# A macaron layer on one core: when PE ranks the tokens of batch 2, and whether VectorE adds the mix before or after its side piece

## The reference

```python
def attn(x):
    Q, K, V = (jnp.einsum('bne,hde->hbnd', x, W) for W in (Wq, Wk, Wv))
    scores = jnp.einsum('hbnd,hbmd->hbnm', Q, K) * scale
    w = jax.nn.softmax(scores, axis=2)
    mean = jnp.mean(jnp.einsum('hbnm,hbmd->hbnd', w, V), axis=0)
    return mean @ fc_w.T + fc_b
def ffn(x):
    scores = sigmoid(x @ gate_w)
    _, selected = top_k(scores + expert_bias, 2)   # weights: scores of the two, normalised
    shared = silu(x @ shared_gate_w) * (x @ shared_up_w) @ shared_down_w
    for e in range(16):
        routed = routed + comb[:, e:e+1] * (silu(g_e(x)) * u_e(x) @ experts_down[e])
    return shared + routed
x = x + 0.5 * ffn(layernorm(x))
x = x + attn(layernorm(x))
x = x + 0.5 * ffn(layernorm(x))
```

## Time and profile before

| | |
|---|---|
| median of 3 runs | 512.28 us (509.96, 512.28, 513.18) |
| the profiled execution | 512.53 us, of which its span is 511.3 us |
| PE busy in the span | 442.7 us, 87% |
| granted TensorE clock, mean | 0.956 of full speed |
| attention stage | about 165 to 396 us of the span |

### The profile page before, as it was taken

One profiled execution on the slowest core, in us unless ns is written; L12 is line 12 of the kernel. 1 busy time (PEld: TensorE's weight loads), 2 busy tenths in 40 slices (PEclk: granted clock), 3 DMA queues, 4 the chain that ended last, 5 costly groups with the idle time before them and its releaser, 6 DMA issues. The chain is left out here.

```text
span 511.3 us, 10128 instructions
## 1 busy us (share of the span) xinstructions
PE 442.7 (87%) x2951; PEld 394.0 (77%) x2951; DVE 342.4 (67%) x1053; ACT 265.7 (52%) x708; POOL 278.3 (54%) x322
## 2 busy tenths in 40 slices
PE   1676799999787899999999999989979888999982
PEld 1345699899666789988889888979868677899972
DVE  6589575565448575458646875675685786777778
ACT  4855376676523455543544454435434663577750
POOL 5267875565064643386344746738657167266660
PEclk9977699999989999999999999999998988999995
DMA  8672375576632100011000111104001466366968
GB/s 295 242 226 92 114 210 160 189 207 130 160 94 63 53 21 1 1 52 35 28 12 22 53 31 50 57 3 141 31 33 62 153 222 213 102 189 188 303 227 254
DMA packets 44468, 60.33 MB, mean 118 GB/s; under 512 B 6080, under 2 KB 36800, under 8 KB 44416
## 3 DMA queue, kind: packets, MB, share of 16 engines
q1 hardware_dynamic: 34688, 37.11, 23.2%
q0 software_dynamic: 7584, 20.98, 13.7%
q10 hardware_dynamic: 2144, 1.60, 1.0%
HBM read 34.75 MB, written 24.91 MB: 117 GB/s over the span
## 5 line engine op out<-in xcount | busy, mean ns | idle before, releaser
L2099 POOL TENSOR_TENSOR e_sp<-raw,e_sp 128x512 fp32r<-128x512 f32 x48 | 62.2, 1296 | 69.5 <-ACT e_sp L1163 69.0
L400 PE MATMUL bank<-v_sp,e_sp 128*128 128x256 f32 x576 | 78.1, 286 | 2.4 <-DVE x_sb L1703 2.0
L400 PEld LDWEIGHTS bank<-v_sp,e_sp 128*128 128x128 f32 x576 | 75.4, 193 | 6.2 <-issue 2.8
L400 PE MATMUL bank<-g_sp,xT 128*128 128x512 f32 x288 | 75.5, 398 | 0.1
L2063 POOL DMA_INDIRECT raw<-xn_dram,gather_at x47 | 45.6, 971 | 30.9 <-PE bank L406 27.1
L2025 POOL DMA_INDIRECT pair_dram<-raw,slot_i x47 | 45.8, 974 | 30.1 <-ACT raw L1055 26.7
L1186 ACT ACTIVATE raw<-bank,softmax_row 128x512 f32<-128x512 f32 x48 | 33.2, 691 | 55.1 <-DVE softmax_row L1854 54.7
L400 PEld LDWEIGHTS bank<-g_sp,xT 128*128 128x128 f32 x288 | 52.0, 190 | 9.5 <-issue 0.2
L400 PE MATMUL bank<-w_hi,e_sp 128*128 x188 | 51.6, 297 | 1.2 <-DVE e_sp L1672 1.1
L1854 DVE TENSOR_REDUCE softmax_row<-bank 128x1 f32<-128x512 f32 x48 | 32.9, 686 | 25.8 <-PE bank L400 25.3
L1672 DVE TENSOR_TENSOR e_sp<-bank,e_sp 128x128 fp32r<-128x128 f32 x94 | 27.2, 290 | 31.8 <-ACT e_sp L1025 31.1
(11 more groups left out here) (287 smaller groups left out, 1089.6 us busy)
## 6 DMA issues: line engine op xcount, KB each, us to landing
stage<-slab_dram SPq DMA_DIRECT2D x47, 136.0 KB
y_dram<-stage SPq DMA_DIRECT2D x47, 128.0 KB, 3.0
late_pair<-pair_dram SPq DMA_DIRECT2D x16, 256.0 KB, 4.3
slab_dram<-stage SPq DMA_DIRECT2D x17, 136.0 KB
stage<-in_w_pack SPq DMA_DIRECT2D x6, 384.0 KB, 4.9
stage_more<-in_w_pack SPq DMA_DIRECT2D x6, 384.0 KB, 3.2
x_sb<-in_x SPq DMA_DIRECT2D x4, 512.0 KB, 7.0
xn_dram<-xn_all SPq DMA_DIRECT2D x4, 512.0 KB, 5.2
```

The costliest lines, as they stand in the source:

```text
L400: m = pe.matmul(dst, lhs[k][l], rhs[k][r], start=(first and k == 0 and i == 0), stop=(last and k == n - 1 and i == 2), skip_group_check=True)
L2099: pool.tensor_tensor(e_sp[:, i, 1, :], e32[:, i, :], e_sp[:, i, 0, :].bitcast(F32), ALU.subtract).then_inc(s_e_lo, 1)
```

## The change

Four edits, all of them in the order of instructions; none is added or removed.

1. PE, batch 3: `rank_again(2)` moves from slot 13 to slot 14, that is from behind the values of unit 42 to behind the late mix in unit 43. `pack_table(False)` moves from slot 18 (unit 45) to slot 20 (unit 46).
2. DVE, batch 3: `write_table(False)` moves from the start of slot 19 to slot 20, behind the second part of `list_rest`.
3. DVE: the `memset` of `full_cap` moves from slot 15 of batch 3 to the last slot of batch 1.
4. DVE, second unit of batches 1, 2 and 3 (`turn_of_batch`): `attn_out` comes directly behind the maximum, and the side piece moves from there to behind v_lo. In batches 1 and 2 that side piece is `combine` and `norm_stats`; in batch 3 it is `measure`, which stood behind `attn_out` already.

```diff
@@ previous_front of pe_program
                 yield from prev_front(b - 1)
-                for _ in range(2 if b < B - 1 else 3):
+                for _ in range(2 if b < B - 1 else 4):
                     yield
                 rank_again(b - 1)
                 yield
                 if b == B - 1:
-                    for _ in range(4):
+                    for _ in range(5):
                         yield
                     pack_table(False)
                     yield
@@ previous_front of dve_program
                 count_class(b - 1)
+                if b == 1:
+                    chained(dve.memset(full_cap[:], float(FULL_TILES * P)))
                 yield
                 if b == B - 1:
-                    chained(dve.memset(full_cap[:], float(FULL_TILES * P)))
                     chained(dve.memset(list_first[:, LISTED:], 2.0 * E * SLAB))
@@
                     rest = list_rest()
                     next(rest)
                     yield
+                    next(rest)
+                    yield
                     write_table(False)
-                    next(rest)
-                    yield
                     next(rest)
                     yield
@@ the loop over units of dve_program
-                if b + 1 < B:
+                turn_of_batch = b > 0 and u % PER_BATCH == 1
+                if b + 1 < B and not turn_of_batch:
                     side_pieces(u, b, attn_side, ffn_side)
                 if late is not None:
                     attn_out(late)
-                if b + 1 == B:
+                if b + 1 == B and not turn_of_batch:
                     side_pieces(u, b, attn_side, ffn_side)
                 slab_side(u, b, 0)
@@
                 if u == LAST_FOLD_UNIT:
                     fold_split(len(folds) - 1)
+                if turn_of_batch:
+                    side_pieces(u, b, attn_side, ffn_side)
                 side_pieces_late(u, b, ffn_side)
```

More of the change, by code:

```diff
@@ L1737, in previous_front @@
                     yield
-                    write_table(False)
                     next(rest)
                     yield
+                    write_table(False)
                     next(rest)
```

## The result

The changed kernel takes 514.47 us (median of 15 runs, 512.39 to 517.12), the kernel before, run beside it, 512.16 us (15 runs). The ratio is 1.0047, 95% interval 1.0025 to 1.0069: slower by 2.3 us, where 1.0 us faster was forecast. The profiled span is 513.3 us against 511.3 us. PE is still busy for 442.7 us of it; what grew is the time in which it waits.

The account below looks back on a forecast made before the run. PE, busy for 87% of the span, was taken as the place to win time, with DVE and POOL limiting what its 5.6 us of waits yield. -1.1 + 0.5 - 0.4 = -1.0 us gave 511.3 us, range 508.8 to 513.5.

Parts of the forecast that it names:

- Term 1: First mixes of batches 1 and 2: earlier additions remove PE's waits, winning 0.6 and 0.5 us, -1.1 us in all.
- It does the same work between two maxima, so that of unit 14 stays at 227.35: DVE in batch 1: despite the swapped order, the maximum of unit 14 starts at its old time, without idle time ahead.
- the later one blocks: L1343 in batch 3: of a two-SBUF-input VectorE and an SBUF-reading GpSimd instruction, the later waits for the other's end.
- Term 2: Unit 37: moving `measure` delays POOL's root and the normalised tile; PE waits 2.28 us against 1.39, +0.89 us.
- the clock falls in unit 38: Rival, batch 3: after the new 2.28 us wait PE loses up to 1.6 us more; 511.9 us, chance 0.22.
- Terms 2 and 3 together: Batch 3 to unit 43: the rank's 0.95 us wait goes, but DVE's L1343 ends later behind POOL's L2019; +0.5 us.
- Term 4: From unit 43 on: the memset leaves DVE, -0.1 us, and e_lo of unit 47 regains 0.27 us slack; -0.4 us.
- pack_table at nothing: End of batch 3: PE's 2.69 us wait at `pack_table` goes, but its removal wins nothing.
- The sum: Whole kernel: -1.1 + 0.5 - 0.4 = -1.0 us, giving a median of 511.3 us.

Follow-up runs that it names:

- small_elo: Changed kernel with edit 4 in batches 1 and 2 alone and POOL's e_lo of units 13 and 25 cut from 512 to 32 columns: 509.72 us, one run.
- skip_slot: Changed kernel without edit 4, no side piece on any engine in units 13 and 25, later pieces one unit later: 508.51 us, 0.9918 of the kernel before.
- add_first: Changed kernel with additions, then side piece, then reciprocal in batches 1 and 2, old order in batch 3: 515.83 us, 1.0079 of the kernel before.
- filler: Changed kernel with 18 further 128x256 matmuls on PE in the wait of unit 38, their result overwritten: 513.96 us, 1.0061 of the kernel before.
- pack_only: Kernel before with only pack_table and write_table moved to slot 20, the rank in its old slot: 511.03 us, ratio 1.0012.
- rank_only: Kernel before with the rank moved to slot 14 and nothing else: 511.61 us, ratio 1.0009.

## Why the prediction was wrong

**Term 1 failed (-1.1 us forecast, +1.33 measured).** The step is "It does the same work between two maxima, so that of unit 14 stays at 227.35". The list of instructions was the same, but not their time. The waits of the mixes went whole, as forecast, and PE did run ahead (-1.18 us at unit 14); then DVE was 1.0 us later than before, and PE waited 1.14 and 0.34 us. small_elo shows that e_lo makes 0.95 us of this in batch 1. Without it the term is -0.49 there, near the forecast -0.6. For batch 2 it is -0.13 against -0.5, by the idle 0.46 us that stays unexplained. I had laid the moved instructions beside PE's rows and DVE's, and not beside POOL's of the same moment: e_lo of unit 13 starts at 226.03 in the kernel before (225.52 after), and the combines' new place, had they kept their length, is 225.7 to 226.8 after. The block was weighed for L1343, which the change doesn't move, and not for the instruction that it does. POOL before, unit 13:

```profile
226.03 1.28 POOL L2099 TENSOR_TENSOR e_sp<-raw,e_sp 128x512 fp32r<-128x512 f32 x1
```

The trace before even had the size. In unit 1 two combines already ran into an e_lo and took 1.70 us in place of 1.06; DVE, then POOL:

```profile
169.75 1.70 DVE L1575 SCALAR_TENSOR_TENSOR x_sb<-stage,weight,x_sb 128x256 f32<-128x256 f32 x2
```

```profile
169.31 1.28 POOL L2099 TENSOR_TENSOR e_sp<-raw,e_sp 128x512 fp32r<-128x512 f32 x1 [3.78 <-ACT e_sp L1163]
```

The Trainium skill has it, on the page "SBUF — State Buffer", section "Who interferes with whom": a VectorE instruction that reads two SBUF inputs and a GpSimd instruction that reads SBUF exclude each other. The trace agrees for the combine, whose two inputs are both in SBUF: in unit 25 the first takes 1.47 us beside e_lo and 0.48 in small_elo. It agrees too for v_lo, which has one input in PSUM: 0.48 us at 226.21 in skip_slot, with e_lo from 225.72 to 227.01.

The prediction's "the later one blocks" doesn't hold by the starts in these traces. In add_first the second combine of unit 13 starts at 226.12, 0.42 us ahead of e_lo (226.54), and it is the one that takes 2.00 us. What is the same in units 13 and 25 of both kernels is the end: the long combine ends 0.29 us behind e_lo. In unit 1, where it starts 0.44 us behind e_lo, it takes 1.12 us and ends 0.28 us behind it.

**Term 2 was right** in mechanism and size: +0.89 us forecast, and 0.87 us in filler, where the clock doesn't fall; the wait of PE 2.34 us against 2.28.

**The rival "the clock falls in unit 38" came true**, which had a chance of 0.22. It costs PE 1.5 us (1.6 at most forecast) and the end 0.61 us (0.6 forecast), by filler. In the attention stages of all the traces it fell at each wait of PE of 2.15 us or more (2.15 and 2.25 in add_first, 2.34 after, 2.7 at `pack_table`), and at none of up to 1.81 us (filler, ahead of the values of unit 44).

**Terms 2 and 3 together** were +0.5 us, with DVE's L1343 held by POOL's `back_lo` once more. The rows of after, POOL then DVE, show it: the one ends at 368.22, the other at 368.44. L1343 is 2.0 to 2.1 us for the first of its two instructions here in every trace, and 0.22 us in the other batches. That `back_lo` is the cause rests on these times and wasn't tried by itself.

```profile
365.84 2.38 POOL L2023 TENSOR_TENSOR xT<-xT 128x1024 fp32r<-128x1024 f32 x1
```

```profile
366.19 2.25 DVE L1343 TENSOR_TENSOR route<-expert_no,top_at 128x64 f32<-128x64 f32 x2
```

The rank's wait goes, and PE wins 1.19 us up to unit 43 with edit 4 and without it. But where the clock doesn't fall, in filler, PE is 0.31 us early in batch 3 at unit 43 (1.02 - 1.33), then waits for v_lo and is 0.50 us late at unit 44 (1.83 - 1.33): the forecast size, one unit later than I had put it.

**Term 4 was too large.** From unit 44 to the end filler wins 0.10 us, not 0.4: the memset's part came, and the 0.27 us of slack of e_lo did not; it waits 0.29 us for ACT in the kernel after. In unit 23 the memset costs 0.07 us, as allowed for.

**pack_table at nothing was right:** in pack_only the wait of 2.69 us is gone, and from unit 43 to the end of the stage the shift goes from -0.19 to -0.18.

**The sum.** From -1.0 to +2.34 are 3.3 us: 2.4 by term 1 (of which the block is 1.95), 0.6 by the clock, 0.3 by term 4. The range's upper end, 513.5, took in the clock but no loss in batches 1 and 2: term 1 had 0 as its upper end. The number that was missing is what a combine loses beside e_lo: 0.95 us in unit 13 and 0.99 us in unit 25 (1.43 and 1.47 us in place of 0.48), and 1.5 us in add_first, where it starts sooner. The length of e_lo was there to be read in the earlier trace rows, and its place and the collision of unit 1 in the trace.

## What to carry to other kernels

Before an instruction with two SBUF inputs is moved on VectorE, look at what GpSimd reads in that moment: the same two instructions took 1.06 or 2.02 us by their place alone. A wait of PE that goes is worth only what the engine behind it can follow; here 2.69 us were worth nothing. Where a moved chain adds a wait on PE, look in the traces for the waits at which the clock fell, in this kernel those of 2.15 us or more, and count the clock as a cost of its own.

## What the runs showed of the hardware

- The same 12 matmuls of 128x512 took 3.00 us after a wait of 1.39 us and 4.33 us after one of 2.34 us; with PE at work in that wait, 3.00 us.
- The same wait at `pack_table` (2.69 and 2.67 us) went with 3.4 us at the lower clock in the kernel before and 6.8 us in rank_only, where PE came to it 1.4 us sooner. That took 1.2 us back between the values of units 45 and 46. It is one trace of each.
- A `scalar_tensor_tensor` of 128x256 on DVE with both inputs in SBUF took 0.48 us alone, and 1.12 to 2.00 us beside POOL's e_lo, whether it started up to 0.44 us behind e_lo or up to 0.42 us ahead of it; it ended 0.28 to 0.29 us behind e_lo each time.
- The normalised tile (L1250), 0.41 us in the median, took 2.02 us in unit 38 after (347.00 to 349.02), and 1.92 us before (344.62 to 346.54). Both times it began about 0.5 us ahead of POOL's e_lo and ended 0.17 us behind it (e_lo ends at 348.85 and 346.37). It has one large input in SBUF. What holds it was not tried.

```profile
347.00 2.02 DVE L1250 TENSOR_SCALAR raw<-x_sb,moments,rstd 128x256 f32<-128x256 f32 x1
```

```profile
347.56 1.29 POOL L2103 TENSOR_TENSOR e_sp<-raw,e_sp 128x512 fp32r<-128x512 f32 x1
```
